# New instruction orders for PE, ACT, DVE and POOL in a fused gated-delta-attention and feed-forward kernel

## The chip, the cores and the metric

The kernel runs on one core of one Trainium2 chip. The time is that of the device from the first to the last instruction of one execution, in microseconds (us). PE is TensorE, ACT ScalarE, DVE VectorE, POOL GpSimd, SP SyncE. All engines run their own list of instructions in the order in which the kernel issues them, and meet through semaphores. Most matmuls are in float32.

## The reference

For x of shape (2, 4096, 512), with xn the layer norm of x over its last axis, the result is

`out = x + attention(xn) + ffn(xn)`

- **Attention** (4 heads of 128). q, k, v are projections of xn, each followed by a causal convolution of 4 taps and SiLU. beta is a sigmoid of a small projection. The delta rule works in chunks: with normalised k, the strictly lower triangle of k k^T scaled by beta is inverted, the state S is subtracted (y = v - k S), solved for u, and o = q S + (q k^T) u, S = S + k^T u.
- **Convolutions** of v over three lengths (3, 15 and 31 taps per channel), mixed by two matrices (ms_out).
- **Gates.** A two-layer network with GELU sees xn and the mean absolute values of ms_out, o and v, and gives a softmax over three parts. The weighted sum of ms_out, o and v is RMS-normalised and projected by Wo.
- **ffn.** sigmoid(xr Wr) * (relu(xk Wk)^2 Wv), where xr and xk mix xn with its predecessor in time.

## The kernel before, in words

**Tiles.** The sequence is cut into NS = 32 tiles of 128 time steps; a tile holds both batches (NB = 2, b = 0, 1), so most right-hand sides are 256 columns wide. All weights stay in SBUF.

**The loop.** `for i in range(NS + 2)` stands in each engine's program, with three flags: `f` (i < NS), `k` and `c` (i >= 2). In one turn, f works on tile i (layer norm, transposes `turn_x`, projections 0 to 3 of six pairs: v, v, k, k, q, q), k on tile i - 1 (projections 4 and 5, short convolutions, tap convolutions of heads 0 to 3, the inverse), c on tile i - 2 (the rest of the inverse, state, ffn, features, gates, output). A turn in the steady middle is called a stage here.

**The order.** No scheduler runs: each program ends in a list of calls of small helper functions, one list an engine, written out by hand or by a planner (PE from L681, ACT from L1170, DVE from L1550, POOL from L396). A helper waits for the semaphores that its operands and its destination need, issues a few instructions, and counts up its own semaphore. An engine that waits holds up all that stands behind it in its list.

**PE.** `inverse_W(l)` (L500, L504) and `inverse_Z(l)` (L521, L526, L528) build the inverse level by level: each has 64 matmuls of 32x32 by 16 columns, each of these with its own weight load. Between them DVE's `mask_W`, `step_Y` and `turn_Y` (L1426, L1434, L1438, L1415) must run. `inverse_W(0)` waits for `scale_B(1)` on ACT and for `make_aT(0)` on DVE, since it writes the bank `cell[0]` that `query_key(0)` (L483) has filled. `query_key(0)` waits for `scale_B(0)`. `kernel_mix(h)` (L614) multiplies the finished taps of head h; it waits for them and for `copy_mix(h - 1)`, which empties its bank. `key_state`, `solve`, `outputs`, `state` are L554, L561, L568 and L569, L575. `turn_features` (L631) turns the features for `hidden` (L645, L648) once `feature_low` (L1504, DVE) is done. `turn_x` is L426, `project` L439, `turn_o` L670, `attend` L678, `turn_tokens` L468.

**ACT.** `copy_beta` (L905), `tanh_beta` (copy L911, tanh L915), then DVE's `beta_half` and `gains` lead to `scale_B` (L931). `copy_logits` (L1123) empties the logits for `turn_logits` (L663); `exp_logits` (L1127) needs the Exp table. The features go `copy_ms(1)`, `feature_high` (L1093), DVE's `feature_rest` (L1498), `feature_mid` (L1099), `feature_low`. Silu (`short_silu`, L873), Gelu (`gelu_hidden`, L1116) and Exp each need a table; the compiler puts a load (ACT_TABLE_LOAD) where the table at hand does not hold the next function. `copy_raw` (L835) empties a projection's bank for the next but one.

**Taps.** Most taps are DVE instructions (`taps(s, h, lo, hi)`, L1488), some are products on ACT (`first_taps` L1054, `multiply_taps` L1065) that POOL adds by DMA (`add_taps`, L388). `first_taps(2)` waits for `kernel_mix(0)`. The first DVE tap of head 2 waits for `add_taps(2, 0)` to have landed, that of head 3 for `add_taps(3, 3)`.

**SP** loads the next x (L326, 512 KB) as soon as `turn_x(1)` of the tile before is done, and copies x to the output once the tile of two turns before has been stored.

Of the kernel before, what the change touches and what calls it, by code (L numbers as in the profile page):

```python
# [73 lines left out]
def build(nc, x, out, w):  # L74
    NS = x.shape[1] // P
    with ExitStack() as ctx:
# [271 lines left out]
        def pool_program(e):  # L348
# [47 lines left out]
            for i in range(NS + 2):  # L396
                f, k, c = i < NS, 1 <= i <= NS, i >= 2
                if f:
                    deviation(i)
                if k:  # L400
                    add_taps(i - 1, 2, 0)
                    add_taps(i - 1, 3, 0)
                    add_taps(i - 1, 3, 1)
                if c:
                    invert_o(i - 2, 0)
                    invert_o(i - 2, 1)
                if k:
                    add_taps(i - 1, 3, 2)
                    add_taps(i - 1, 3, 3)
                    norms_q(i - 1)  # L410
                    norms_k(i - 1)
                if c:
                    add_out(i - 2)

        def tensor_program(e):
# [265 lines left out]
            for i in range(NS + 2):  # L681
                f, k, c = i < NS, 1 <= i <= NS, i >= 2
                if c:
                    turn_tokens(i - 2, 3)
                    inverse_Z(i - 2, 5)
                    ffn_key(i - 2, 0)
                    half_W(i - 2)
                    ffn_key(i - 2, 1)
                    half_X(i - 2)
                    ffn_out(i - 2, 0)  # L690
                    solve(i - 2, 1)
                    key_state(i - 2, 0)
                    kernel_mix(i - 2, 2)
# [14 lines left out]
                if c:  # L708
                    turn_features(i - 2)
                    hidden(i - 2, 0)  # L710
                    hidden(i - 2, 1)
                if k:
                    turn_tokens(i - 1, 0)
                if c:
                    hidden(i - 2, 2)
# [9 lines left out]
                if k:  # L725
                    gram(i - 1, 0)
                if c:
                    turn_logits(i - 2)
                if k:
                    turn_beta(i - 1)  # L730
                    kernel_mix(i - 1, 0)
                    gram(i - 1, 1)
                    query_key(i - 1, 0)
                if f:
                    turn_x(i, 0)
                if k:
                    turn_tokens(i - 1, 2)
                    inverse_W(i - 1, 0)
                    query_key(i - 1, 1)
# [18 lines left out]
                if k:  # L758
                    inverse_Z(i - 1, 3)
                if f:  # L760
                    project(i, 3)
                if c:
                    turn_o(i - 2, 0)
                if k:
                    inverse_W(i - 1, 4)
                if c:
                    turn_o(i - 2, 1)
                    attend(i - 2, 0)
                if k:
                    inverse_Z(i - 1, 4)  # L770
                if c:
                    attend(i - 2, 1)
                if k:
                    inverse_W(i - 1, 5)

        def scalar_program(e):
# [393 lines left out]
            for i in range(NS + 2):  # L1170
                f, k, c = i < NS, 1 <= i <= NS, i >= 2
                if c:
                    relu_key(i - 2, 0)
                    copy_mix(i - 2, 1)
                    square_key(i - 2, 0)
                if k:
                    short_first(i - 1, 0)
                if c:
                    scale_v(i - 2, 1)
                if f:  # L1180
                    sum_x(i)
                if k:
                    copy_raw(i - 1, 2)
                if c:
                    relu_key(i - 2, 1)
                    square_key(i - 2, 1)
                    join_half_X(i - 2)
                    copy_u(i - 2, 1)
                if k:
                    short_first(i - 1, 1)  # L1190
                    take_raw_halo(i - 1, 3)
                    take_raw_halo(i - 1, 4)
                if c:
                    copy_u(i - 2, 0)
                    tanh_gate(i - 2, 0)
                if k:
                    odd_ones(i - 1)
                if c:
                    copy_o(i - 2, 0)
                    copy_o(i - 2, 1)  # L1200
                    copy_mix(i - 2, 2)
                    tanh_gate(i - 2, 1)
                if k:
                    copy_raw(i - 1, 3)
                if c:
                    copy_mix(i - 2, 3)
                if k:
                    short_first(i - 1, 2)
                    short_first(i - 1, 3)
                    take_raw_halo(i - 1, 5)  # L1210
                    short_silu(i - 1, 0)
                    copy_raw(i - 1, 4)
                    short_first(i - 1, 4)
                if f:
                    take_raw_halo(i, 0)
                if c:
                    copy_ms(i - 2, 0)
                    copy_ms(i - 2, 1)
                    feature_high(i - 2)
                    feature_mid(i - 2)  # L1220
                if k:
                    short_silu(i - 1, 1)
                    short_silu(i - 1, 2)
                    copy_raw(i - 1, 5)
# [11 lines left out]
                if k:  # L1236
                    shift(i - 1)
# [4 lines left out]
                if k:  # L1242
                    square_q(i - 1)
                if c:
                    gelu_hidden(i - 2, 2)
                if k:
                    multiply_taps(i - 1, 2, 0)
                    copy_tokens(i - 1, 1)
                if c:
                    gelu_hidden(i - 2, 3)  # L1250
                if f:
                    square_x(i)
                if c:
                    copy_logits(i - 2)
                if k:
                    copy_beta(i - 1)
                if c:
                    exp_logits(i - 2)
                if k:
                    tanh_beta(i - 1)  # L1260
                if f:
                    normalize(i, 0)
# [581 lines left out]
```

How the kernel before makes its waits and increments, by code:

```python
        def sync_program(e):  # L284
# [6 lines left out]
            def load_projections():  # L291
                load(v_in, wv[:, :, :], by_rows(w["wv"]))
                for j, n in enumerate(("cv", "ck", "cq")):
                    load(v_in, cw[:, j, :, :], w[n].rearrange("(c p) k -> p c k", p=P))
                load(k_in, wk[:, :, :], by_rows(w["wk"]))
                load(q_in, wq[:, :, :], by_rows(w["wq"]))
                e.wait_ge(zeroed, N_ZEROED)
                load(q_in, wb[:, :, 0:H], by_rows(w["wb"]))
# [24 lines left out]
            def load_x(s):  # L323
                if s:
                    e.wait_ge(*x_turned.upto(s - 1))
                e.dma_start(xa[:, :, :], x[:, s * P:(s + 1) * P, :].rearrange("b p d -> p b d")).then_inc(xa_in, 16)
# [1 line left out]
            def copy_x(s):  # L328
                if s >= 2:
                    e.wait_ge(stored[s % 2], s // 2 * 16)
                e.dma_start(out[:, s * P:(s + 1) * P, :], x[:, s * P:(s + 1) * P, :]).then_inc(x_copied[s % 2], 16)
# [3 lines left out]
            load_projections()  # L336
            load_convolutions()
            load_x(1)
            load_rest()
            for i in range(NS + 2):
                if 2 <= i < NS:
                    load_x(i)
                if 1 <= i <= NS:
                    copy_x(i - 1)
            for i in range(2):
                e.wait_ge(stored[i], NS // 2 * 16)
# [1 line left out]
        def pool_program(e):  # L348
# [2 lines left out]
                e.memset(t, 0.0).then_inc(zeroed, 1)  # L351
            e.wait_ge(zeroed, N_ZEROED)
            e.wait_ge(cst_in, 16)
```

## Time and profile before

| | us |
|---|---|
| median of 3 runs | 3585.44 |
| lowest, highest | 3582.49, 3594.63 |
| the profiled execution | 3585.26 |
| its span, first to last instruction | 3583.2 |
| PE busy in the span | 3454.6 (96%) |
| DVE busy | 3199.5 (89%) |
| ACT busy | 2765.0 (77%) |
| POOL busy | 423.0 (12%) |

How to read it: busy times are those of one execution. The time around the span is 2 us, so a change of the span is a change of the time. Matmuls overlap each other and their weight loads, so a row of n matmuls ends a little before start plus length, and the start of the next row is the better mark. "Idle before" is time in which the engine had nothing to run; "issue" means that no semaphore that the profile shows was behind it.

### The profile page before, as it was taken

The page shows a single profiled execution, that of the slowest core. Times are in us where ns is not written, and L with a number is a line of the kernel's source. Part 1 is how long each engine was busy: PE and PEld are TensorE (multiplying, and loading weights), DVE is VectorE, ACT ScalarE, POOL GpSimd, SP SyncE. Part 2 cuts the span into 40 slices and gives each one's busy share as a digit, 9 for nine tenths or more (in the row PEclk, how much of TensorE's full clock was granted, in tenths as well). Part 3 has the DMA queues.
Part 4 walks back from the last instruction along what each step waited for, and adds up shares of the span by engine and source line. Part 5 has one row for each costly group of instructions (what it writes and reads, how often), then busy time and mean ns, then how long its engine had stood idle before and what let it go on. Part 6 is the DMA issues. An engine that isn't in the chain of part 4 may idle for free. (4 is left out here: it accounts for less than half of the span.)

```text
span 3583.2 us, 97697 instructions
## 1 busy us (share of the span) xinstructions
PE 3454.6 (96%) x37184; PEld 2572.7 (72%) x37184; DVE 3199.5 (89%) x8208; ACT 2765.0 (77%) x9176; POOL 423.0 (12%) x497
## 2 busy tenths in 40 slices
PE   6999999999999999999999999999999999999986
PEld 5677777777777777777777777777777777777764
DVE  6998898998989999989999989989999998899983
ACT  5677887778887778887788877788877788777774
POOL 1011100111100111101111001111001110011110
PEclk9999999999999999999999999999999999999988
DMA  5022111122111122111221111221112221112110
GB/s 177 5 41 42 35 31 28 31 41 42 30 32 25 38 42 40 31 28 26 41 42 37 30 28 31 41 41 30 32 22 41 42 38 29 31 27 41 36 26 10
DMA packets 52204, 131.04 MB, mean 37 GB/s; under 512 B 9389, under 2 KB 9901, under 8 KB 51481
## 3 DMA queue, kind: packets, MB, share of 16 engines
q0 software_dynamic: 31744, 79.70, 12.9%
q1 hardware_dynamic: 19992, 45.10, 3.7%
q8 instruction: 294, 4.82, 0.6%
q14 instruction: 174, 1.42, 0.1%
HBM read 45.09 MB, written 33.55 MB: 22 GB/s over the span
## 5 line engine op out<-in xcount | busy, mean ns | idle before, releaser
L1488 DVE SCALAR_TENSOR_TENSOR my<-vT,mw,my 128x256 f32<-128x256 f32 x5408 | 2230.9, 480 | 105.6 <-ACT my L1054 69.9
L645 PE MATMUL dense<-xsh,w 128*128 128x256 f32 x2048 | 481.9, 381 | 1.3
L645 PEld LDWEIGHTS dense<-xsh,w 128*128 128x128 f32 x2048 | 368.3, 190 | 68.9 <-ACT xr L1116 8.3
L388 POOL DMA_DIRECT2D my<-prod x160 | 141.8, 886 | 964.6 <-ACT my L1054 498.4
L439 PE MATMUL front<-xsh,wk 128*128 128x256 f32 x1024 | 239.9, 387 | 3.4 <-ACT raw L835 3.4
L439 PE MATMUL front<-xsh,wv 128*128 128x256 f32 x1024 | 240.9, 388 | 0.8 <-ACT xsh L812 0.8
L586 PE MATMUL dense<-xk,wfk 128*128 128x256 f32 x1024 | 239.5, 387 | 0.0
L357 POOL TENSOR_SCALAR vare<-xsq 128x2 f32<-128x2 f32 x32 | 6.1, 192 | 1951.3 <-ACT xsh L797 1951.3
L678 PE MATMUL dense<-wo,ms 128*128 128x512 f32 x512 | 235.7, 604 | 0.0
L598 PE MATMUL dense<-wr,xr 128*128 128x512 f32 x512 | 233.7, 599 | 1.2 <-DVE xb L1471 1.2
L1065 ACT ACTIVATE prod<-vT,mw 128x256 f32<-128x256 f32 x480 | 210.3, 511 | 28.2 <-DMA my<-prod 27.9
L439 PE MATMUL front<-xsh,wq 128*128 128x256 f32 x1024 | 231.9, 379 | 0.0
L602 PE MATMUL dense<-wfv,ka 128*128 128x512 f32 x512 | 230.2, 592 | 0.0
L623 PE MATMUL dense<-cm,ym 128*128 128x512 f32 x512 | 225.0, 592 | 0.0
L439 PEld LDWEIGHTS front<-xsh,wq 128*128 128x128 f32 x1024 | 191.9, 190 | 38.8 <-issue 14.8
L990 ACT ACTIVATE Bm<-cell,g 128x128 f32<-128x128 f32 x256 | 73.0, 368 | 184.7 <-PE cell L561 184.7
L439 PEld LDWEIGHTS front<-xsh,wk 128*128 128x128 f32 x1024 | 190.1, 190 | 29.9 <-ACT raw L835 3.5
L439 PEld LDWEIGHTS front<-xsh,wv 128*128 128x128 f32 x1024 | 190.7, 191 | 27.9 <-issue 1.4
L586 PEld LDWEIGHTS dense<-xk,wfk 128*128 128x128 f32 x1024 | 190.3, 191 | 27.0
L614 PE MATMUL small<-my,km 128*128 128x256 f32 x768 | 201.8, 400 | 2.2 <-issue 2.2
L1054 ACT ACTIVATE my<-vT,mw 128x256 f32<-128x256 f32 x384 | 167.4, 507 | 36.2 <-PE small L614 35.9
L602 PEld LDWEIGHTS dense<-wfv,ka 128*128 128x128 f32 x512 | 97.2, 190 | 122.5 <-issue 108.6
(181 smaller groups left out, 6897.8 us busy)
## 6 DMA issues: line engine op xcount, KB each, us to landing
my<-prod POOLq DMA_DIRECT2D x160, 384.0 KB, 4.1
xa<-in_x SPq DMA_DIRECT2D x32, 512.0 KB, 4.2
out<-xb POOLq DMA_DIRECT2D x32, 512.0 KB, 5.9
w<-in_w SPq DMA_DIRECT2D x1, 2048.0 KB, 17.1
wv<-in_wv SPq DMA_DIRECT2D x1, 1024.0 KB, 6.6
wk<-in_wk SPq DMA_DIRECT2D x1, 1024.0 KB, 8.9
wq<-in_wq SPq DMA_DIRECT2D x1, 1024.0 KB, 8.4
wfk<-in_wfkT SPq DMA_DIRECT2D x1, 1024.0 KB, 7.1
```

The source lines that it names most:

```text
L388: e.dma_start(my[h % 2][:, :, :], prod[:, :, :], accum_op=ALU.add).then_inc(taps_added, 16)
L439: i = e.matmul(by_batch(front[pair % 2][:, c * W:(c + 1) * W]), wt[:, k, hs(c0 + c)], xsh[s % 2][:, k, :, 1:1 + P], start=(k == 0), stop=( ...
L586: i = e.matmul(dense[pair][:, c * W:(c + 1) * W], wfk[:, k, hs(2 * pair + c)], xk[:, k, :], start=(k == 0), stop=(k == CB - 1))
L598: i = e.matmul(dense[0][:, :], xr[:, k, hs(b)], wr[:, k, :], start=(k == 0), stop=(k == CB - 1))
L602: i = e.matmul(dense[1][:, :], ka[:, k, hs(b)], wfv[:, k, :], start=(k == 0), stop=(k == CB - 1))
L614: i = e.matmul(s_mix, km[:, p, :], my[h % 2][:, p, :], start=(p == 0), stop=(p == 2))
L623: i = e.matmul(dense[b][:, :], ym[:, k, hs(b)], cm[:, k, :], start=(k == 0), stop=(k == CB - 1))
L645: e.matmul(by_batch(o), w1[:, k, hs(2 * pair + c)], xsh[s % 2][:, k, :, 1:1 + P], start=(k == 0), stop=False)
L678: i = e.matmul(dense[b][:, :], ms[:, b, hs(h)], wo[:, h, :], start=(h == 0), stop=(h == H - 1))
L1054: i = e.activation(by_batch(my[h % 2][:, p, :]), vT[s % 2][:, c, :, VH - TAPS[j] + 1:VH - TAPS[j] + 1 + P], ACT.Copy, scale=mw[:, WOFF[j] ...
L1065: i = e.activation(by_batch(prod[:, p, :]), vT[s % 2][:, c, :, off:off + P], ACT.Copy, scale=mw[:, col:col + 1])
L1488: i = e.scalar_tensor_tensor(o, vT[s % 2][:, c, :, off:off + P], mw[:, col:col + 1], o, ALU.mult, ALU.add)
```

## The change

The same helpers are called in another order on PE, ACT, DVE and POOL; the helpers, their waits, the buffers and SP's list are the same. The part of the inverse from `inverse_Z(5)` to `half_X`, `ffn_key` and `ffn_out(0)` are called at the end of a turn for tile i - 1, no more at the start of the next one for tile i - 2. `norms_q` is called for tile i - 2 at the start of POOL's turn. Some runs of `taps` are cut or joined in other places; each tap is still called once a tile. Below are POOL and PE whole, ACT from `short_first(2)` to the end of the turn, and three places of DVE, with 12 columns of indentation taken off.

```diff
@@ -395,19 +395,22 @@
 
 for i in range(NS + 2):
     f, k, c = i < NS, 1 <= i <= NS, i >= 2
+    if c:
+        norms_q(i - 2)
     if f:
         deviation(i)
     if k:
         add_taps(i - 1, 2, 0)
         add_taps(i - 1, 3, 0)
+    if c:
+        invert_o(i - 2, 0)
+    if k:
         add_taps(i - 1, 3, 1)
-    if c:
-        invert_o(i - 2, 0)
+        add_taps(i - 1, 3, 2)
+    if c:
         invert_o(i - 2, 1)
     if k:
-        add_taps(i - 1, 3, 2)
         add_taps(i - 1, 3, 3)
-        norms_q(i - 1)
         norms_k(i - 1)
     if c:
         add_out(i - 2)
@@ -681,16 +684,9 @@
 for i in range(NS + 2):
     f, k, c = i < NS, 1 <= i <= NS, i >= 2
     if c:
-        turn_tokens(i - 2, 3)
-        inverse_Z(i - 2, 5)
-        ffn_key(i - 2, 0)
-        half_W(i - 2)
-        ffn_key(i - 2, 1)
-        half_X(i - 2)
-        ffn_out(i - 2, 0)
+        kernel_mix(i - 2, 2)
+        key_state(i - 2, 0)
         solve(i - 2, 1)
-        key_state(i - 2, 0)
-        kernel_mix(i - 2, 2)
         solve(i - 2, 0)
     if k:
         project(i - 1, 4)
@@ -708,10 +704,10 @@
     if c:
         turn_features(i - 2)
         hidden(i - 2, 0)
+    if k:
+        turn_tokens(i - 1, 0)
+    if c:
         hidden(i - 2, 1)
-    if k:
-        turn_tokens(i - 1, 0)
-    if c:
         hidden(i - 2, 2)
     if k:
         turn_tokens(i - 1, 1)
@@ -723,25 +719,22 @@
         logits(i - 2, 0)
         logits(i - 2, 1)
     if k:
+        turn_beta(i - 1)
         gram(i - 1, 0)
+        turn_tokens(i - 1, 2)
     if c:
         turn_logits(i - 2)
     if k:
-        turn_beta(i - 1)
-        kernel_mix(i - 1, 0)
         gram(i - 1, 1)
         query_key(i - 1, 0)
+        kernel_mix(i - 1, 0)
+        inverse_W(i - 1, 0)
     if f:
         turn_x(i, 0)
-    if k:
-        turn_tokens(i - 1, 2)
-        inverse_W(i - 1, 0)
+        turn_x(i, 1)
+    if k:
+        inverse_W(i - 1, 1)
         query_key(i - 1, 1)
-    if f:
-        turn_x(i, 1)
-    if k:
-        inverse_W(i - 1, 1)
-        key_state(i - 1, 1)
         inverse_Z(i - 1, 1)
         kernel_mix(i - 1, 1)
         inverse_W(i - 1, 2)
@@ -757,21 +750,31 @@
         project(i, 2)
     if k:
         inverse_Z(i - 1, 3)
+    if c:
+        turn_o(i - 2, 0)
+    if k:
+        key_state(i - 1, 1)
+    if c:
+        attend(i - 2, 0)
+    if k:
+        inverse_W(i - 1, 4)
     if f:
         project(i, 3)
     if c:
-        turn_o(i - 2, 0)
-    if k:
-        inverse_W(i - 1, 4)
-    if c:
         turn_o(i - 2, 1)
-        attend(i - 2, 0)
     if k:
         inverse_Z(i - 1, 4)
+        turn_tokens(i - 1, 3)
     if c:
         attend(i - 2, 1)
     if k:
         inverse_W(i - 1, 5)
+        ffn_key(i - 1, 0)
+        inverse_Z(i - 1, 5)
+        ffn_key(i - 1, 1)
+        half_W(i - 1)
+        ffn_out(i - 1, 0)
+        half_X(i - 1)
 
         def scalar_program(e):
 e.wait_ge(zeroed, N_ZEROED)
@@ -1169,151 +1172,160 @@
...
         short_first(i - 1, 2)
+        take_raw_halo(i - 1, 5)
         short_first(i - 1, 3)
-        take_raw_halo(i - 1, 5)
         short_silu(i - 1, 0)
+    if c:
+        copy_ms(i - 2, 0)
+    if k:
         copy_raw(i - 1, 4)
+        short_silu(i - 1, 1)
         short_first(i - 1, 4)
-    if f:
-        take_raw_halo(i, 0)
-    if c:
-        copy_ms(i - 2, 0)
+    if c:
         copy_ms(i - 2, 1)
         feature_high(i - 2)
         feature_mid(i - 2)
-    if k:
-        short_silu(i - 1, 1)
+    if f:
+        take_raw_halo(i, 0)
+    if k:
+        take_v_halo(i - 1)
         short_silu(i - 1, 2)
+    if c:
+        copy_features(i - 2)
+    if k:
         copy_raw(i - 1, 5)
-    if c:
-        copy_features(i - 2)
-    if k:
-        take_v_halo(i - 1)
         short_first(i - 1, 5)
+        short_silu(i - 1, 3)
         first_taps(i - 1, 0)
-        short_silu(i - 1, 3)
         short_silu(i - 1, 4)
         short_silu(i - 1, 5)
     if c:
         gelu_hidden(i - 2, 0)
     if k:
-        shift(i - 1)
         first_taps(i - 1, 1)
         copy_tokens(i - 1, 0)
     if c:
         gelu_hidden(i - 2, 1)
     if k:
         square_q(i - 1)
+        copy_tokens(i - 1, 1)
+        multiply_taps(i - 1, 2, 0)
     if c:
         gelu_hidden(i - 2, 2)
-    if k:
-        multiply_taps(i - 1, 2, 0)
-        copy_tokens(i - 1, 1)
-    if c:
         gelu_hidden(i - 2, 3)
+    if k:
+        copy_beta(i - 1)
     if f:
         square_x(i)
+    if k:
+        tanh_beta(i - 1)
     if c:
         copy_logits(i - 2)
     if k:
-        copy_beta(i - 1)
-    if c:
-        exp_logits(i - 2)
-    if k:
-        tanh_beta(i - 1)
+        scale_B(i - 1, 0)
+        scale_B(i - 1, 1)
     if f:
         normalize(i, 0)
-    if k:
-        scale_B(i - 1, 0)
+        normalize(i, 1)
+    if k:
         first_taps(i - 1, 2)
-        scale_B(i - 1, 1)
+    if c:
+        exp_logits(i - 2)
     if f:
-        normalize(i, 1)
         copy_xnT(i, 0)
-    if c:
-        weigh_delta(i - 2, 0)
+        copy_xnT(i, 1)
     if k:
         copy_mix(i - 1, 0)
     if c:
         weigh_ms(i - 2, 0)
-    if f:
-        copy_xnT(i, 1)
-    if c:
-        weigh_delta(i - 2, 1)
     if k:
         multiply_taps(i - 1, 3, 0)
         first_taps(i - 1, 3)
     if c:
-        weigh_v(i - 2, 0)
-        weigh_ms(i - 2, 1)
-        weigh_v(i - 2, 1)
-        square_o(i - 2, 0)
+        weigh_delta(i - 2, 0)
     if f:
         take_raw_halo(i, 1)
-    if k:
-        multiply_taps(i - 1, 3, 1)
+    if c:
+        weigh_v(i - 2, 0)
+        weigh_delta(i - 2, 1)
     if f:
         copy_raw(i, 0)
     if c:
-        square_o(i - 2, 1)
+        square_o(i - 2, 0)
+    if k:
+        multiply_taps(i - 1, 3, 1)
+    if c:
+        weigh_ms(i - 2, 1)
+        normalize_o(i - 2, 0)
+    if k:
+        copy_tokens(i - 1, 2)
+    if c:
+        weigh_v(i - 2, 1)
+        copy_oT(i - 2, 0)
     if f:
         copy_raw(i, 1)
     if k:
+        multiply_taps(i - 1, 3, 2)
+    if c:
+        square_o(i - 2, 1)
+    if k:
         mix_half(i - 1)
-        multiply_taps(i - 1, 3, 2)
-    if f:
-        take_raw_halo(i, 2)
-    if c:
-        normalize_o(i - 2, 0)
+    if c:
         normalize_o(i - 2, 1)
-        copy_oT(i - 2, 0)
+    if k:
+        multiply_taps(i - 1, 3, 3)
+    if c:
         copy_oT(i - 2, 1)
     if k:
-        multiply_taps(i - 1, 3, 3)
-        copy_tokens(i - 1, 2)
-        copy_W(i - 1)
         spread_X(i - 1)
-        join_X(i - 1)
-        copy_tokens(i - 1, 3)
-        scale_v(i - 1, 0)
-        copy_half_W(i - 1)
@@ -1554,76 +1566,87 @@
     if i == 2:
         prepare_weights()
     if c:
+        taps(i - 2, 3, 0, 2)
+        taps(i - 2, 3, 3, 4)
+        taps(i - 2, 3, 2, 3)
+        taps(i - 2, 2, 48, 49)
+        taps(i - 2, 3, 5, 6)
+        taps(i - 2, 3, 4, 5)
...
-        taps(i - 2, 3, 30, 31)
+        taps(i - 2, 3, 32, 34)
+        taps(i - 2, 3, 35, 37)
+        gate_value(i - 2, 0)
+        subtract_state(i - 2, 0)
+        taps(i - 2, 3, 39, 40)
         taps(i - 2, 3, 38, 39)
-        taps(i - 2, 3, 40, 41)
-        taps(i - 2, 3, 33, 34)
-        taps(i - 2, 3, 41, 42)
-        subtract_state(i - 2, 0)
-        taps(i - 2, 3, 36, 37)
...
+        taps(i - 2, 3, 72, 78)
+    if k:
+        short_conv(i - 1, 0)
+    if c:
+        gate_value(i - 2, 1)
+    if k:
+        short_conv(i - 1, 1)
+        short_conv(i - 1, 2)
     if f:
         negate_mean(i)
-    if c:
-        taps(i - 2, 3, 47, 48)
-        taps(i - 2, 3, 43, 44)
-        taps(i - 2, 3, 42, 43)
-        taps(i - 2, 3, 50, 51)
-        taps(i - 2, 3, 45, 47)
-        taps(i - 2, 3, 48, 50)
-        taps(i - 2, 3, 51, 52)
-        taps(i - 2, 3, 53, 55)
-        taps(i - 2, 3, 52, 53)
-        taps(i - 2, 3, 56, 57)
...
```

## Rows read from the trace of the kernel before

**Rows 1.** The page: busy time of each engine, and the queue of instructions.
```profile
PE 3454.6 (96%) x37184; PEld 2572.7 (72%) x37184; DVE 3199.5 (89%) x8208; ACT 2765.0 (77%) x9176; POOL 423.0 (12%) x497
...
q8 instruction: 294, 4.82, 0.6%
```

**Rows 2.** Windows: length, busy us of each engine (count), granted clock, DMA share, GB/s.
```profile
177.26:3447.56 3270.30, 3218.25 (x34861) 2398.82 (x34861) 2986.78 (x7679) 2586.70 (x8601) 392.60 (x448) 1.00 0.17 34
944.28:1051.58 107.30, 106.68 (x1162) 79.63 (x1163) 99.44 (x257) 86.18 (x288) 13.22 (x15) 1.00 0.17 35
286.13:398.18 112.05, 109.76 (x1162) 81.83 (x1162) 99.92 (x257) 86.31 (x288) 13.18 (x15) 0.97 0.17 33
292.94:299.76 6.82, 6.52 (x141) 5.25 (x141) 4.88 (x13) 2.75 (x8) 0.00 (x0) 0.50 0.13 49
```

**Rows 3.** Waits of PE: for whom, us in total, times, longest us.
```profile
PE cell L521 <- issue: 15.6, 14, 1.4
...
PE cell L500 <- issue: 12.1, 16, 1.5
PE cell L483 <- ACT Bm L931: 11.8, 32, 0.6
```

**Rows 4.** Timeline of PE in one steady stage: start, us, instruction, [idle before].
```profile
2030.89 1.16 PE L483 MATMUL cell<-qT,kT 128*128 128x128 f32 x8 [0.36 <-ACT Bm L931]
...
2033.11 0.73 PE L500 MATMUL cell<-cst,Bm 32*32 32x16 f32 x64 [0.19 <-ACT Bm L931]
...
2035.95 1.16 PE L554 MATMUL cell<-S,kT 128*128 128x128 f32 x8
...
2047.81 0.73 PE L500 MATMUL cell<-Yq,Bm 32*32 32x16 f32 x64
```

**Rows 5.** Timeline of PE: gaps inside groups of matmuls, in two stages.
```profile
293.24 1.86 PE L554 MATMUL cell<-S,kT 128*128 128x128 f32 x7 [1.68 <-issue]
...
1927.86 0.36 PE L500 MATMUL cell<-Yq,Bm 32*32 32x16 f32 x20 [0.95 <-issue]
...
1932.14 0.49 PE L500 MATMUL cell<-Yq,Bm 32*32 32x16 f32 x35 [0.33 <-issue]
```

**Rows 6.** Timeline of ACT: table loads and beta's tanh, first and steady stage.
```profile
33.70 1.28 ACT L873 ACT_TABLE_LOAD   x1
...
52.76 0.21 ACT L915 ACTIVATE bt<-bq 128x8 f32<-128x8 f32 x1
...
2027.29 1.28 ACT L1127 ACT_TABLE_LOAD   x1
...
2028.90 0.21 ACT L915 ACTIVATE bt<-bq 128x8 f32<-128x8 f32 x1
```

**Rows 7.** Timelines of ACT, DVE and PE around the features.
```profile
2007.61 0.72 ACT L873 ACTIVATE vT<-vT 128x256 f32<-128x256 f32 x2
...
2007.73 0.23 DVE L1504 TENSOR_TENSOR fparts<-frest,fparts 128x72 bf16<-128x72 f32 x1 [0.32 <-ACT fparts L1099]
...
2008.16 0.27 PE L631 MATMUL small<-ident,fparts 128*108 128x128 bf16 x2
```

**Rows 8.** Timelines of POOL and DVE: issue of add_taps(2,0), first tap that needs it.
```profile
2032.33 0.94 POOL L388 DMA_DIRECT2D my<-prod  x1 [4.49 <-ACT my L1054]
...
2036.59 1.27 DVE L1488 SCALAR_TENSOR_TENSOR my<-vT,mw,my 128x256 f32<-128x256 f32 x3
...
399.61 0.94 POOL L388 DMA_DIRECT2D my<-prod  x1 [4.49 <-ACT my L1054]
...
405.59 1.28 DVE L1488 SCALAR_TENSOR_TENSOR my<-vT,mw,my 128x256 f32<-128x256 f32 x3 [0.24 <-DMA my<-prod]
```

**Rows 9.** Timelines of ACT, PE and DVE in the first turn with k.
```profile
75.52 1.31 ACT L1065 ACTIVATE prod<-vT,mw 128x256 f32<-128x256 f32 x3 [9.30 <-DMA my<-prod]
...
77.41 5.41 PE L439 MATMUL front<-xsh,wk 128*128 128x256 f32 x16 [3.40 <-ACT raw L835]
...
83.53 0.29 DVE L1438 TENSOR_TENSOR Yq<-Yq,cell 128x128 f32<-128x128 f32 x1 [4.98 <-PE cell L521]
```

More of the change, by code:

```diff
@@ L714, in tensor_program @@
                 if c:
+                    hidden(i - 2, 1)
                     hidden(i - 2, 2)
@@ L743, in tensor_program @@
                     inverse_W(i - 1, 1)
-                    key_state(i - 1, 1)
+                    query_key(i - 1, 1)
                     inverse_Z(i - 1, 1)
@@ L1198, in scalar_program @@
                 if c:
+                    scale_v(i - 2, 1)
+                if k:
+                    copy_raw(i - 1, 2)
+                    short_first(i - 1, 1)
+                if c:
+                    copy_half_W(i - 2)
+                if k:
+                    take_raw_halo(i - 1, 3)
+                if c:
+                    relu_key(i - 2, 1)
+                    copy_mix(i - 2, 1)
+                if k:
+                    shift(i - 1)
+                    take_raw_halo(i - 1, 4)
+                if c:
+                    square_key(i - 2, 1)
+                    tanh_gate(i - 2, 0)
+                    scale_v(i - 2, 0)
+                    join_half_X(i - 2)
+                    copy_u(i - 2, 1)
+                    copy_mix(i - 2, 2)
+                    copy_u(i - 2, 0)
                     copy_o(i - 2, 0)
                     copy_o(i - 2, 1)
-                    copy_mix(i - 2, 2)
-                    tanh_gate(i - 2, 1)
                 if k:
@@ L1205, in scalar_program @@
                 if c:
+                    tanh_gate(i - 2, 1)
                     copy_mix(i - 2, 3)
@@ L1702, in vector_program @@
                 if k:
+                    taps(i - 1, 2, 10, 11)
+                    taps(i - 1, 2, 17, 18)
+                    taps(i - 1, 2, 15, 16)
+                    taps(i - 1, 2, 13, 14)
+                    step_Y(i - 1, 2)
+                    taps(i - 1, 2, 20, 21)
+                    turn_Y(i - 1, 3)
+                    taps(i - 1, 2, 18, 19)
+                    taps(i - 1, 2, 23, 24)
+                    taps(i - 1, 2, 21, 22)
+                    taps(i - 1, 2, 24, 25)
                     taps(i - 1, 2, 16, 17)
+                    taps(i - 1, 2, 26, 27)
+                    mask_W(i - 1, 3)
                 if c:
@@ L1734, in vector_program @@
                     taps(i - 1, 2, 33, 34)
+                    step_Y(i - 1, 3)
+                    taps(i - 1, 2, 36, 37)
                     taps(i - 1, 2, 40, 41)
+                    turn_Y(i - 1, 4)
+                    taps(i - 1, 2, 41, 42)
+                    taps(i - 1, 2, 31, 32)
+                    taps(i - 1, 2, 42, 43)
+                    mask_W(i - 1, 4)
+                    taps(i - 1, 2, 43, 44)
                     mix_in(i - 1)
-                    taps(i - 1, 2, 41, 42)
+                    step_Y(i - 1, 4)
+                    taps(i - 1, 2, 44, 45)
                     taps(i - 1, 2, 34, 35)
-                    turn_Y(i - 1, 4)
-                    mask_W(i - 1, 4)
-                    taps(i - 1, 2, 42, 43)
-                    taps(i - 1, 2, 36, 37)
-                    taps(i - 1, 2, 43, 45)
+                    taps(i - 1, 2, 45, 46)
+                    taps(i - 1, 2, 37, 38)
+                    taps(i - 1, 2, 46, 47)
+                    turn_Y(i - 1, 5)
                 if c:
```

253 lines of the change are left out of this document (112 added, 141 removed).

## The prediction, made before the changed kernel ran

> **What bounds the kernel now.** The page's first part says TensorE: PE is busy 96% of the span, DVE 89%, ACT 77% [rows 1]. The windows then say how full PE is where it matters. A stage is one turn of the loop over i; the 30 from 177.26 to 3447.56 take 3270.30 us with 3218.25 of PE work [rows 2]: 109.0 us a stage. The undisturbed stage from 944.28 takes 107.30 with 106.68 of PE work, the one from 286.13 takes 112.05 for the same 1162 matmuls. So a new order can win at most what stands between PE's work and the stage, not the matmuls' own time; and DVE and ACT, with 99.4 and 86.2 us of work a stage, are not the bound unless PE has to wait for one of them.
>
> PE's list of waits says what stands there [rows 3]. Two waits come in each stage: query_key(0) for scale_B(0), 11.8 us in 32 [rows 3], and inverse_W(0) for scale_B(1); read in a stage they are 0.36 and 0.19 [rows 4], 0.55 us together. The others are "issue": 15.6 us in 14 and 12.1 us in 16 on the 32x16 matmuls, with two smaller groups some 35 us, or 1.1 a stage. These stop in the middle of a group that no semaphore guards. The queue of kind "instruction" moved 4.82 MB in 294 packets [rows 1], so one packet is 16.4 KB, and PE's 74,368 instructions over 294 are 253: a packet is some 256 of them. Between the two gaps of one stage, at 1927.86 and 1932.14, lie 127 matmuls, each with its weight load, and a few waits: 256 again [rows 5]. So I read the gaps as PE running out of instructions. There it used up 256 in 4.0 us and then waited 0.33: a packet takes about 4.3 us to come, and only where inverse_W and inverse_Z put 128 instructions into 0.7 us [rows 4] is PE faster than that. Behind the gap of 1.68 us at 293.24 the granted clock is 0.50 (1.2 of 2.4 GHz) from 292.94 to 299.76 [rows 2, 5].
>
> The Trainium skill ("Runtime: NRT & Kernel Launch", Instruction fetch mechanics) has the fetch of the next 256 instructions mostly hidden, with PE's buffer at 2048; by that a denser order costs nothing and (f) below would be 0; the gaps of this trace speak against it.
>
> **The change, part by part.** No instruction, wait or buffer is added. Much of the diff is where the loop's body is cut: ffn_key, half_W, ffn_out(0), half_X move from the top of one turn to the bottom of the one before, which is the same place. I compare the order as a cycle. Costs are per steady stage, times 30.
>
> (a) *The beta chain.* copy_beta and tanh_beta now stand ahead of copy_logits and exp_logits, turn_beta ahead of gram(0), scale_B(1) ahead of first_taps(2). Before, the table load at 2027.29 (1.28 us) stood in front of tanh_beta at 2028.90, because exp_logits did [rows 6]. Without it, with square_x (1.4) in its place, beta's tanh comes at about 2027.4, scale_B(0) ends at 2029.05 and scale_B(1), no more behind 1.2 us of first_taps, at 2030.1. query_key(0) is ready for them at 2029.6, inverse_W(0) after kernel_mix(0) at 2032.0. Both waits go: -0.55 x 30 = -16.5 us. This rests on tanh needing no table load behind Gelu. No row shows tanh there; rows show it without a load behind Exp (2028.90) and behind Silu (52.76, the last load at 33.70) [rows 6], so I take none. Bounds: none, or 0.9 us of wait per stage (rival 3).
>
> (b) *short_silu(1) moves ahead of copy_ms(1)*, so ahead of the features; take_raw_halo(0) (0.1) goes behind. Features run on ACT without a gap and are 0.62 - 0.1 = 0.52 later, as silu(1) begins now after them at 2007.61 and takes 0.62. feature_low ended at 2007.96 and turn_features began on PE at 2008.16 [rows 7]: 0.20 of slack, less 0.06 for the semaphore. PE then waits 0.38 us in each stage; nothing else is ready, since project(5) is used up. +11.4. Bounds 0 to 0.5.
>
> (c) *kernel_mix(1) behind copy_mix(0).* kernel_mix(0) went from before gram(1) to after query_key(0) and ends at 2032.0; first_taps(2) waits for it (1.3), then the exp table load (1.28), two copy_xnT (1.0) and copy_mix(0): done at 2036.05. PE comes to kernel_mix(1) at 2035.9, having lost key_state(1) (1.1 [rows 4]) from the stretch. +0.2: +6. Bounds 0 to 0.5.
>
> (d) *Near ties.* solve(0) has only solve(1) (0.89) to cover subtract_state(0) (0.69 plus 0.25 of semaphores), kernel_mix(3) has one more tap ahead of it, attend(0) comes 0.1 before copy_oT(0). 0.25 together: +7.5. Bounds 0 to 0.5.
>
> (e) *The tap additions.* DVE's first tap of head 2 needs add_taps(2,0) landed. Before, POOL issued it at 2032.33 and DVE used it without a wait at 2036.59 (4.26 or less); in another stage issue to tap was 5.98 with DVE waiting (399.61 to 405.59) [rows 8]. Now first_taps(2) ends 1.4 later, so the issue is at 2033.7, and turn_x(1) starts x's 512 KB load at the same time, not 3 us later: both on the same engines. From the landing to inverse_W(3), DVE has 17 taps at 0.4 (three in 1.28 [rows 8]), mask_W(2), add_two, add_three and step_Y(2): 8.4 us. inverse_W(3) stood at 2047.81 [rows 4] and is due at 2046.2 now, 12.5 after the issue, so the landing may take 4.1. Between 4.2 and 6.0 the wait is 0.1 to 1.9, less the 1.1 us that PE loses to instructions in the same stretch anyway. I take 0.5: +15. Bounds 0 and 1.9 x 30.
>
> (f) *Instruction supply.* The dense stretch loses key_state(1) and the two waits, but kernel_mix(0) stands close ahead and turn_x(0) and (1) are inside it. I laid 256-instruction windows over both orders with the durations above: the shortest holds 2.2 us of work in both. +0.1: +3. Bounds -0.3 to +0.5 a stage, the falls of the clock with it: the stage with the gap of 1.68 is 4.75 longer than the undisturbed one [rows 2], so 3 us of it are the clock's.
>
> (g) *Both ends.* In the first stage with k, multiply_taps(3,1) waits 9.30 us for a DMA, copy_raw(0) stands behind it, so PE waits 3.40 and DVE 4.98 [rows 9]. copy_raw(0) is ahead now, and DVE, which bounds this stage up to solve(0), gains 4. In the last two turns weigh, square and normalize of batch 0 go ahead of batch 1: 1 us off the end, and 1 in the stage without f, which DVE's length sets. -6. Bounds -10 to 0. POOL's norms_q goes behind add_out and is due only at copy_o of the next turn; SP issues the same transfers in the same order.
>
> Sum: -16.5 + 11.4 + 6 + 7.5 + 15 + 3 - 6 = +20.4. The profiled execution took 3585.26 us (span 3583.2), the median of the runs 3585.44, so both bases agree: about **3605 us**.
>
> **The rivals.**
> 1. *Faster.* If (b) to (e) are covered, as (e) is where the add lands in 4.1 us and (b) where ACT is half a microsecond ahead, only (a) and (g) stay: 3585.3 - 22.5 = 3563. For it: four of my terms are differences of two long sums that come out within 0.5 us. Against: (b) is a plain shift against a slack that is read directly. It decides at 0.2 us of delay of the features. Chance 0.25.
> 2. *No change.* PE's supply of instructions sets the stretch: what the two waits no longer take, the next packet takes, and the tap additions hide in the same gap. Then (a) and (e) are 0, (b) and (g) stay with half of (c) and (d): about +10, or 3590 with its neighbours 3577 to 3595. That from project(4) to hidden(0) PE's order as a cycle is the old one, so that the change does less than the diff's length says, speaks for it too; against it, (b) lies outside the dense stretch. Chance 0.32.
> 3. *A table load in front of tanh_beta.* Then copy_logits comes at 2029.05, turn_logits, now ahead of gram(1), waits 0.9 us: +27 on the sum, 3632. Against it are the rows of (a). Chance 0.08, inside slower. 
>
> **How the numbers follow.** The forecast (slower by over 0.3%, 10.8 us, about what a measurement can tell) has 0.43 with rival 3, no change 0.32, faster 0.25. The low end is rival 1's 3563, with 0.1 us a stage of (b) to (e) left: 3566. The high end is the sum with (e) at 1.2 and (c), (d) at 0.4: 3605 + 21 + 6 + 5 = 3637, rounded to 3640.
>
> **What would show it.** (a): no wait of query_key(0) or inverse_W(0) for ACT's scale_B, 96 table loads as before with the Exp one at exp_logits. (b): turn_features waits for DVE's feature_low in each stage, 0.3 to 0.5. (c): kernel_mix(1) waits for copy_mix. (e): DVE's waits for the tap DMA grow from 28.8 us to over 40, and inverse_Z(2) or inverse_W(3) waits for DVE. (f): issue gaps stay near 35 us. (g): no wait of 3.4 us for copy_raw in the first stage. The prediction is wrong if PE's waits in a steady stage sum to under 0.55 us, or if issue gaps leave the range of 25 to 50.

## The result and the profile after

The changed kernel takes **3628.44 us** (median of 6 runs, 3622.01 to 3633.99) against 3585.06 (6 runs) for the kernel before: ratio **1.0119**, 95% interval 1.0103 to 1.0134, so 43 us slower. Forecast were 3605, with 3566 to 3640 as range. The profiled execution took 3630.37 us, its span is 3628.6.

Page of the changed kernel, busy time of each engine [rows 1] (lines of the kernel's file are some 3 to 12 higher than before):

```profile
PE 3466.4 (96%) x37184; PEld 2569.2 (71%) x37184; DVE 3205.2 (88%) x8208; ACT 2787.0 (77%) x9176; POOL 468.6 (13%) x497
```

The work is the same; PE's 12 us more go with a lower mean granted clock, 0.983 against 0.987. Waits of PE [rows 3]: for whom, us in total, times, longest:

```profile
PE cell L524 <- DVE Wq L1438: 39.9, 20, 11.5
PE cell L503 <- issue: 30.5, 19, 2.9
...
PE cell L503 <- DVE Yq L1450: 10.6, 16, 3.8
PE small L617 <- issue: 8.6, 1, 8.6
...
PE small L617 <- ACT ym L1075: 4.3, 13, 0.4
...
PE small L634 <- DVE fparts L1516: 3.3, 2, 3.0
```

The 8.6 us at L617 are one wait of kernel_mix before the first outputs, from 121.26 to 129.82 us. No packet of q8, the queue of instructions, starts in it. DVE is in its taps all that time and ends one at 129.72. So it is most likely a wait for taps that the profile gives no semaphore for:

```profile
117.76 12.36 DVE L1500 SCALAR_TENSOR_TENSOR my<-vT,mw,my 128x256 f32<-128x256 f32 x31
```

The two waits for scale_B are gone. In their place inverse_Z waits for mask_W (L1438), inverse_W for step_Y (L1450). DVE's own waits name what stands behind both (28.8 us in 37 before, 2.3 the longest):

```profile
DVE my L1500 <- DMA my<-prod: 80.7, 37, 12.6
```

Where the time went, from the first matmul of outputs(0) in each turn: the first comes at 139.22 us (130.69 before), the last at 3552.47 (3508.38), the end at 3628.57 (3583.18). So the head costs 8.5 us more, the 31 turns between 35.6 (1.15 each), the tail 1.3.

Within a stage I took each of PE's calls from its first matmul to that of the next call, averaged over 27 stages. This step also holds waits that the idle column shows only in part, as matmuls in flight cover them. Worked out from PE's rows, in us:

| step of PE | before | after | first run below | what follows it |
|---|---|---|---|---|
| project(0) | 3.66 | 4.96 | 3.82 | inverse_Z(2), waits for mask_W(2) |
| inverse_W(2) | 0.93 | 1.67 | 1.14 | "issue" inside it |
| project(1) | 3.66 | 4.10 | 3.76 | inverse_W(3), waits for step_Y(2) |
| project(5) | 3.46 | 3.72 | 3.72 | turn_features |
| gram(1) | 1.42 | 0.97 | 0.97 | query_key(0), waited for scale_B(0) |
| turn_tokens(2) | 0.79 | 0.44 | 0.44 | before: inverse_W(0), waited for scale_B(1) |
| whole stage | 109.02 | 110.36 | 108.47 | |

One stage shows the mechanism. Timelines of SP, POOL, DVE and PE of the changed kernel, then its DMA view for the same two issues (last column: median us from issue to landing):

```profile
2395.32 0.38 SPq L326 DMA_DIRECT2D xa<-in_x  x1
...
2395.49 0.93 POOL L388 DMA_DIRECT2D my<-prod  x1 [5.33 <-ACT my L1057]
...
2398.90 0.45 DVE L1427 STREAM_TRANSPOSE Xq<-Yq 128x256 f32<-128x256 f32 x1
2401.31 3.25 DVE L1500 SCALAR_TENSOR_TENSOR my<-vT,mw,my 128x256 f32<-128x256 f32 x8 [1.97 <-DMA my<-prod]
2404.49 0.28 DVE L1438 TENSOR_TENSOR Wq<-cell,cst 128x128 f32<-128x128 f32 x1
...
2403.00 0.25 PE L503 MATMUL cell<-Yq,Bm 32*32 32x16 f32 x7 [2.78 <-issue]
```

```profile
xa<-in_x SPq DMA_DIRECT2D x1, 512.0 KB, 4.1
my<-prod POOLq DMA_DIRECT2D x1, 384.0 KB, 5.7
```

SP and POOL issue within 0.2 us of each other, but SP's packets go first. In the kernel before, the addition issued at 2032.33 [rows 8] landed after 4.0 us by the same view, as the x load came 4.1 us behind it. The records of the packets say how: the x load runs from 2396.35 to 2399.05, the addition from 2398.39 to 2400.93, and while both run the addition's packets in progress rise from 1 to 17 as the load's fall from 15 to none. Over 27 stages the addition's first packet starts 2.96 us after the issue, never under 2.49; without a load in front it is 1.51. Its last packet ends 5.81 us after the issue instead of 4.39, and the semaphore that DVE waits for tells of the landing at 6.18 instead of 4.77 (means). DVE waits 2.2 us a stage for it instead of 0.4. (The expectations below go by 5.8 against 4.2, and by waits of 2.17 against 0.32.)

The Trainium skill ("DMA: Bandwidth & Descriptors", Queues, rings and completion order) has each DMA engine take turns between queues, but drain a whole packet of some 9 to 17 descriptors first. The trace fits this: the load is 272 records, which is 17 for each of 16 engines, and the addition's begin only as the load's run out. The records do not name their engine, so that each engine finishes its 17 first is not shown.

### The profile page after: what moved, and what is told of

Read it like the earlier page. It is cut to its first block, busy times and chain, and to the rows that moved or that the text cites. A ratio compares the mean times of both kernels' runs of the same rounds, so it can differ in the third digit from the quotient of the medians.

```text
span 3628.6 us, 97702 instructions
## 1 busy us (share of the span) xinstructions
PE 3466.4 (96%) x37184; PEld 2569.2 (71%) x37184; DVE 3205.2 (88%) x8208; ACT 2787.0 (77%) x9176; POOL 468.6 (13%) x497
## 3 DMA queue, kind: packets, MB, share of 16 engines
q14 instruction: 173, 1.42, 0.1%
## 4 chain that ended last, share of the span: by engine, by line
PE 71%; ACT 13%; DMA 6%; issue 5%; DVE 4%; ACTq 0%; POOL 0%; POOLq 0%; DVEq 0%; SPq 0%
PE dense L648 12%; PE front L442 11%; PE dense L681 6%; PE dense L601 6%; PE dense L589 6%; PE dense L605 6%; DMA my<-prod 6%; DVE my L1500 3%; PE small L617 3%; PE cell L479 2%; ACT dense L1087 2%; PE turn L471 2%; PE cell L564 2%; PE cell L578 2%; PE cell L572 2%
## 5 line engine op out<-in xcount | busy, mean ns | idle before, releaser
L442 PE MATMUL front<-xsh,wv 128*128 128x256 f32 x1024 | 258.8, 409 | 4.0 <-issue 3.2
L442 PEld LDWEIGHTS front<-xsh,wv 128*128 128x128 f32 x1024 | 203.5, 204 | 36.2 <-issue 4.4
L617 PE MATMUL small<-my,km 128*128 128x256 f32 x768 | 198.9, 395 | 14.7 <-issue 8.6
L626 PEld LDWEIGHTS dense<-cm,ym 128*128 128x128 f32 x512 | 94.8, 190 | 107.1 <-issue 107.1
```

The costliest lines, as they stand in the source:

```text
L442: i = e.matmul(by_batch(front[pair % 2][:, c * W:(c + 1) * W]), wt[:, k, hs(c0 + c)], xsh[s % 2][:, k, :, 1:1 + P], start=(k == 0), stop=( ...
L617: i = e.matmul(s_mix, km[:, p, :], my[h % 2][:, p, :], start=(p == 0), stop=(p == 2))
L626: i = e.matmul(dense[b][:, :], ym[:, k, hs(b)], cm[:, k, :], start=(k == 0), stop=(k == CB - 1))
```

## The experiments

All are timed against the kernel before; the ratio is given with its 95% interval.

### The x load behind the addition

The changed kernel with one wait more, on SP:

```diff
 def load_x(s):
     if s:
         e.wait_ge(*x_turned.upto(s - 1))
+    if s >= 2:
+        e.wait_ge(*adds_before(s - 2, 2, 1))
     e.dma_start(xa[:, :, :], ...)
```

> The new orders, with one wait more on SP: the load of tile s's x also waits until add_taps(2,0) of tile s-2 has landed. Theory T (collision): in the new orders the x load is issued 0.9 us after the issue of add_taps(2,0), so its packets go first, the add lands 5.8 us after its issue and not 4.2, DVE's first tap of head 2 waits 2.17 us a stage and not 0.32, and the head loses 8.5 us in the same way. By T the add lands within 3.9 us again, DVE's waits for the tap DMA fall from 80.7 to under 35 us, PE's waits for DVE's mask_W from 39.9 to under 12, and the time from 3628 to 3570-3585. Rival 1 (features, near ties and the denser instruction stream carry the loss): 3615-3630, whatever DVE waits. Rival 2 (only the head is the collision's): 3618-3622.

Measured: **3561.72 us**, ratio 0.994 (0.9928 to 0.9952), 67 us faster than the changed kernel (64 by the two ratios) and 22 faster than the one before. Waits of PE and DVE, and the DMA view of one addition:

```profile
PE cell L505 <- issue: 16.4, 16, 1.5
...
PE cell L505 <- DVE Yq L1452: 7.0, 6, 4.2
...
PE cell L526 <- DVE Wq L1440: 4.5, 4, 2.5
...
DVE my L1502 <- DMA my<-prod: 15.3, 30, 1.4
```

```profile
my<-prod POOLq DMA_DIRECT2D x1, 384.0 KB, 4.1
```

The addition begins 1.51 us after its issue, its last packet ends after 3.89 and it lands after 4.27 (means). The 31 turns lose 56.4 us of length and the head 7.3 (first outputs at 131.88), so it is the same cause at both places. The time is below the range that I gave: the collision costs 1.8 us a turn, where the difference to the kernel before was 1.15, as it had also eaten a gain of the new orders.

### The x load two additions later

The same wait with `adds_before(s - 2, 3, 2)`.

> As the run before, but the x load waits for the landing of add_taps(3,1), two additions later, so that it falls between two additions and behind the dense stretch of the inverse. If only add_taps(2,0) matters (T): the same as the run before within 5 us. If the x load slowed PE's instruction packets or add_taps(3,0) as well, another 5-15 us faster. If ACT's sum_x of the next turn comes to wait for x (it is due 38 us after the turn's first addition, the load would land some 25 us after it), slower than the run before.

Measured: **3552.60 us**, ratio 0.9914 (0.99 to 0.9928). Another 9 us by the medians, in the bounds given, but the two intervals touch. The profiles show only part of it, and not the part that was put: the head is 3.6 us shorter (first outputs at 128.29), while the 31 turns take as long as in the run before it (3357.4 against 3356.9). PE's "issue" waits sum to 25 us against 32, but that is one wait of kernel_mix in the head (2.6 us, not 8.5); after the first outputs they are 22.1 against 23.2. So the turns show no gain from fewer waits for instructions.

### The same wait on the old orders

> Control: the kernel before, its orders untouched, with the wait of the second run alone (the x load waits for the landing of add_taps(3,1)). Theory T: in the kernel before the x load's packets came 4.1 us after the issue of add_taps(2,0), in the shadow of the addition, and DVE waited only 0.32 us a stage; so this gains 0 to 8 us, 3576-3584, and what the second run won over the kernel before is the new orders' own. Rival: the x load disturbs additions and instruction packets in both kernels, and the second run's gain is the later load's alone: 3550-3562.

Measured: 3584.16 us, ratio 1.0003 (0.9993 to 1.0014). That is the upper edge of what was put. DVE's wait for the additions stays at 32.3 us (28.8 before). The later load by itself is worth nothing; what the two runs above won is the new orders' own.

### The collision on the old orders

The kernel before, its addition held back until the event that releases the x load; and the same with the x load behind the addition.

```diff
 def add_taps(s, h, r):
+    if (h, r) == (2, 0) and s + 1 < NS:
+        e.wait_ge(*x_turned.upto(s + 1))
     e.wait_ge(*tap_zero.upto(s, h))
```

> The converse, on the kernel before: POOL's add_taps(2,0) also waits until turn_x(1) of the same turn is done, the event that releases SP's x load. Nothing else changes. The addition is then issued some 2 us later than before and 0.9 us ahead of the x load's packets, as in the new orders. Theory T (position): it begins 2.7-3.1 us after its issue and lands 5.5-6.0 after it, so 7.5-8 after the old issue instead of 4.2; DVE's wait grows from 0.32 to over 3 us a stage, and the time by 1.5 to 3 us a stage, 3630-3680. Rival (in the old orders the landing has slack enough, so the collision alone costs little): below 3610.

> The run before it with the x load waiting for that addition's landing: the same delay of the issue, without the collision. Theory T: it lands 3.7-3.9 us after its issue, 2 us less than in the run before, and 1 to 2 us a stage come back: 30-60 us faster than that run. Rival (the delay of the issue is all that counts): within 10 us of that run.

Measured: **3720.90** us (1.0392, 1.0374 to 1.041) and **3644.15** (1.0176, 1.0158 to 1.0194); the first and the difference of both are larger than put, though the addition starts 2.52 us after its issue, a little sooner than put. DVE waits 4.9 us a stage for it in the first and 3.5 in the second. Both additions are issued at the same late event, so the 77 us between them are the collision's. The first is 141 us slower than the kernel before, so the delay of the issue costs the other 65. DVE's and PE's waits of the first, then of the second:

```profile
PE cell L502 <- DVE Yq L1440: 125.4, 32, 13.4
...
DVE my L1490 <- DMA my<-prod: 168.6, 48, 14.5
```

```profile
PE cell L504 <- DVE Yq L1442: 72.4, 32, 3.3
...
DVE my L1492 <- DMA my<-prod: 113.7, 42, 4.3
```

Here PE waits for step_Y on DVE (L1440, L1442), which stands behind the tap that needs the addition. An addition that ends 1.5 us later (its last packet 5.53 against 4.05 us after the issue) makes PE's wait for step_Y 53 us longer in 32 turns, and the mean granted clock falls from 0.984 to 0.973 with it.

### The addition made small

The changed kernel; add_taps(2,0) moves `[:, 0:1, 0:16]` of the tile, so most of one product of head 2 is left out.

> The new orders with the early x load as they are, but add_taps(2,0) moves 64 bytes a partition instead of 3072 (it leaves out most of that one addition of products, so the sums of head 2 are incomplete). It tells position from bandwidth. If the addition is late because its packets stand behind those of the x load (position): it still begins 2.5 to 3.1 us after its issue instead of 1.5, lands at 3.2-3.7, DVE's wait shrinks from 2.17 to 0.1-0.3, and the time is 3555-3570. If the addition is late because two transfers share the engines (bandwidth): it begins 1.5 us after its issue. If the landing is not what costs, 3615-3630. Issue gaps of 2.2 to 2.9 us in inverse_W(2) should go in any case if a PE packet stood behind the addition's bytes.

Measured: 3551.72 us, ratio 0.9913 (0.9893 to 0.9934), 3 us below the range put; DVE waits 0.4 us a stage. Waits of PE, and the DMA view of the 32 small additions:

```profile
PE cell L504 <- issue: 11.3, 14, 1.3
...
PE small L618 <- issue: 8.5, 1, 8.5
...
PE cell L525 <- DVE Wq L1439: 3.5, 3, 2.5
```

```profile
my<-prod POOLq DMA_DIRECT2D x32, 8.0 KB, 3.9
```

Even with 64 bytes a partition the first packet starts 2.63 us after the issue (mean of 27; 1.51 in the last two turns, where no x is loaded). So it stands behind the load; its last packet ends after 3.60 us. And the gaps of over 2 us in inverse_W are gone, 1.3 at most: in the changed kernel PE's 16 KB packet of instructions ran from 2400.78 to 2401.76, from the time that the addition's last packets ended (2400.93), and PE went on at 2403.00, 1.24 us after it had come. In this kernel nothing long stands in front of it.

### DVE's inverse steps ahead of the taps

The changed kernel; on DVE mask_W(2) moves up 5 taps and step_Y(2) 4, both still behind the tap that waits.

> The new orders with the early x load and its late addition as they are; on DVE alone mask_W(2) goes 5 taps up and step_Y(2) 4 taps up, both still behind the tap that waits for the addition. If the late landing costs because mask_W(2) and step_Y(2) stand 8 and more taps behind it on DVE: DVE's wait for the addition stays at 2 us a stage, but PE's waits for mask_W fall from 39.9 to under 12 us, and the time to 3575-3600. If PE loses time to the collision in another way (packets of instructions behind the addition, the clock): over 3605, and issue gaps as in the new orders, 45 us.

Measured: 3617.46 us, ratio 1.0102 (1.0083 to 1.0121). That is 11 us under the changed kernel's median, but its interval overlaps that one's (1.0103 to 1.0134), so a gain is not clear of the noise. The time is in the second expectation (over 3605); the waits for mask_W fall, but not to under 12. PE's waits:

```profile
PE cell L503 <- issue: 29.1, 19, 2.7
PE cell L524 <- DVE Wq L1438: 24.5, 18, 9.3
```

The step of project(0) falls from 4.96 to 4.10, but inverse_W(2) stays at 1.71 and project(2) grows by 0.37. So this order on DVE shortens one wait and gives a part of it back at another, and the waits for instructions in inverse_W stay (29.1 against 30.5 us).

### The same, with the late x load

mask_W(2) 2 taps up, on the second run.

> The second run (late x load) with mask_W(2) 2 taps up on DVE. PE waited there 5.4 us in all for mask_W and 16 for instructions in inverse_W. If these are what is left to order: 3-5 us faster than the second run's 3552.6. If DVE then waits for inverse_W(2) instead: the same within 4 us, or slower.

Measured: 3552.18 us, ratio 0.9923 (0.9906 to 0.994): the same as without it.

### The short silu

The changed kernel, and the second run, with one call moved on ACT:

```diff
     copy_raw(i - 1, 4)
-    short_silu(i - 1, 1)
...
+    short_silu(i - 1, 1)
     take_v_halo(i - 1)
     short_silu(i - 1, 2)
```

> The new orders with one call moved on ACT: short_silu(1) goes back behind feature_mid, in front of take_v_halo. Prediction's term (b): 0.25 to 0.38 us a stage, so 7.5 to 11.4 us faster than the new orders, 3617-3621; the step from project(5) to turn_features falls back from 3.72 to 3.46 us. Rival: the DVE wait for the tap addition later in the stage takes it back (the additions hang on ACT too, which would be as late as now): 3625-3630.

> The second run with short_silu(1) back behind feature_mid, so term (b) alone without the collision. In the third run PE's step at project(5) fell by 0.26 us but the one at hidden(1) grew by 0.38, as hidden(2) then waits for gelu_hidden(0). If ACT's work from copy_ms to gelu_hidden(0) is the bound of that stretch whatever its order: the same as the second run within 5 us (3548-3558). Prediction's term (b) as it was put: 8 to 11 us faster, 3542-3545.

Measured: 3628.08 us (1.0125, 1.0112 to 1.0138) and 3559.79 (0.9936, 0.9921 to 0.9952): no gain in either; beside the second run the second one is 7 us slower, and their intervals just overlap. A new line stands among PE's waits of the first:

```profile
PE dense L648 <- ACT xr L1119: 6.4, 30, 0.4
```

The step of project(5) falls from 3.72 to 3.46 as put, but hidden(1)'s grows from 3.69 to 4.06: hidden(2) now waits for gelu_hidden(0) (L1119). All of it, the silu and the features, stands in front of that gelu on ACT.

### The beta chain alone, on the old orders

> The kernel before with the beta chain alone in the new order: copy_beta and tanh_beta ahead of copy_logits and exp_logits, scale_B(1) ahead of first_taps(2), turn_beta ahead of gram(0), turn_tokens(2) in front of turn_logits, exp_logits behind normalize(1), softmax_top and softmax_rest later on DVE. kernel_mix(0), the features and the short silu stay. Prediction's term (a): the waits of query_key(0) and inverse_W(0) for scale_B go, 0.55 us x 30 = 16.5 us, 3565-3572. Rival (supply of instructions): PE runs into the next packet earlier by what it gained, 3580-3588 with issue gaps grown by 10 us or more. Second rival: first_taps(2) comes later (0.9 us) behind scale_B(1), the addition with it, and DVE's waits for the tap DMA grow by over 10 us: 3580-3595.

> The beta chain alone on the kernel before, mended: copy_logits stays ahead of copy_beta and softmax_top ahead of beta_half, so that the bank of the logits is empty for kernel_mix(0) as before. Only exp_logits goes behind normalize(1), scale_B(1) goes ahead of first_taps(2), turn_beta ahead of gram(0), softmax_rest behind mask_W(1), and the two copy_xnT ahead of weigh_delta. Term (a): the 0.55 us a stage of waits for scale_B go, 3565-3573. Rival (instruction supply takes it back): 3580-3586 with the issue gaps grown by some 10 us. Rival (first_taps(2) is 0.9 us later and with it the addition): up to 3590, DVE's waits for the tap DMA over 45 us.

Measured: **3747.82** us (1.0455, 1.044 to 1.0471) and **3660.01** (1.0219, 1.0203 to 1.0235). None of the expectations came, in either run. PE's waits of the first, then of the second:

```profile
PE small L614 <- DVE lg L1514: 88.3, 31, 2.9
PE front L439 <- ACT raw L835: 31.6, 23, 2.2
```

```profile
PE front L456 <- ACT bqT L905: 34.7, 32, 2.5
PE front L439 <- ACT raw L835: 24.3, 18, 4.2
```

In the first, kernel_mix(0) waits for the bank that turn_logits has filled and softmax_top has not yet emptied. In the second, turn_beta (L456) waits for copy_beta, behind square_x and copy_logits on ACT. So neither way of moving the chain alone gives its gain. My reading, which no run took apart: copy_beta first makes the logits late, these need turn_tokens(2) as cover, and kernel_mix(0) must go behind them. That kernel_mix(0) in turn makes first_taps(2) and the addition late.

### The beta chain undone, on the new orders

The second run; on ACT copy_logits and exp_logits in front of tanh_beta, on DVE softmax_top in front of beta_half.

> Term (a) undone on the second run (new orders, late x load): on ACT copy_logits and exp_logits, with its table load, go back in front of tanh_beta, and softmax_top back in front of beta_half on DVE; PE's order stays the new one. If the beta chain is what makes the new orders faster than the old without the collision (31 us in the second run, where the prediction gave (a) 16.5): scale_B(0) ends some 1.3 to 2 us later in each stage, and all or more of the gain goes, 3575-3620, with PE waiting for scale_B in each stage. If the gain lies elsewhere (neighbours of small groups on PE, the ends): 3550-3560.

Measured: 3638.01 us, ratio 1.0158 (1.0137 to 1.0178), 85 us slower than the second run and past the range.

```profile
PE cell L488 <- ACT Bm L936: 61.5, 32, 2.2
```

The step of gram(1) is 3.10 us, not 0.97: query_key(0) waits for a scale_B(0) that has exp_logits in front, with its table load (1.28 us) and its wait for softmax_top. The gain of the new orders hangs on this chain.

## Why the prediction went wrong in size

**Right:** slower, inside the range; and the collision in (e) was named with its cause, x's load at the same time as the addition. That the time is inside the range is in part luck: two errors of opposite sign stand in the sum. The collision was put at 15 us and cost 67 (the first run gives them back), and all the rest was put at +5.4 and is -22, the first run against the kernel before.

- **(e), the term that failed.** The prediction took 0.5 us a stage between bounds of 0 and 1.9. The landing was foreseen between 4.2 and 6.0 us after the issue and came after 6.2 in the mean of 27 stages, 5.7 at the least: the load is always first, and the addition starts as it runs out. By the prediction's own line (the landing may take 4.1) that is a wait of 2.1, "less the 1.1 us that PE loses to instructions in the same stretch anyway". This subtraction is the step that failed. The 1.1 are no cover: PE's packet comes behind the same addition and is later with it; the "issue" waits after the first outputs are 37.5 us with the collision and 23.2 without. The steps of project(0), project(1) and inverse_W(2) cost 1.30 + 0.44 + 0.74 = 2.5 us a stage. Taking the cause away gives back 67 us, 1.8 a turn and 7.3 in the head: close to the upper bound.
- **(a)** was right, and larger: the steps of gram(1) and turn_tokens(2) shrink by 0.45 + 0.35 = 0.80 us where the idle rows showed 0.55; undoing the chain costs 85 us. Tanh behind Gelu needs no load, so rival 3 did not come.
```profile
L1119 ACT ACT_TABLE_LOAD x32 | 41.1, 1283 | 0.6
L1130 ACT ACT_TABLE_LOAD x32 | 41.1, 1283 | 0.6
L876 ACT ACT_TABLE_LOAD x31 | 39.8, 1283 | 0.6
```

- **(b)** has its price, 0.25 us at project(5) instead of 0.38, but it is no loss against another place of the silu, as the two runs show.
- **(c)** did not come: kernel_mix(1)'s step fell from 1.86 to 1.53 us, its waits for copy_mix are 4.3 us in all. **(d)** about as put: solve, kernel_mix(3) and attend(0) are 0.34 longer together, against 0.25.
- **(f)** "Issue" waits are 46 us, not near 35, inside the range of 25 to 50; 8.6 of them are kernel_mix's in the head. After the first outputs they are 37.5 us against 34.2 before, with nine gaps of over 2 us against one. Without the collision they are 23.2, so the new orders alone lose less to them than the old. The length of instruction windows did not foresee either; what grew is the time that a packet takes behind an addition.
- **(g)** Wrong in sign: for the head -4 foreseen and +8.5 measured, for the end -2 foreseen and +1.3 measured behind the last outputs. The timelines of SP, POOL and DVE show why:

```profile
61.69 0.42 SPq L326 DMA_DIRECT2D xa<-in_x  x1
62.16 0.65 SPq L332 DMA_DIRECT2D out<-in_x  x1
...
61.66 1.09 POOL L388 DMA_DIRECT2D my<-prod  x1 [7.51 <-ACT my L1057]
...
77.77 3.26 DVE L1500 SCALAR_TENSOR_TENSOR my<-vT,mw,my 128x256 f32<-128x256 f32 x8 [12.58 <-DMA my<-prod]
```

  SP's copy of x to the output (L332) follows the load at once. By the packet records it runs until 77.18, and the addition's last packets end with it, single ones 2.7 us apart. The wait of 3.4 for copy_raw is gone as put, and with the collision away the first outputs come at 128.29 in the second run, 2.4 earlier than before.

The 3563 of rival 1 is near what the new orders take without the collision, 3561.72, but not for its reasons: (b) and (d) are there, (a) is larger, and (g) gives nothing (head 1.2 us and tail 1.8 us longer than before in the first run). And rival 2's own parts, (b), (g) and half of (c) and (d), sum to +12 or 3597, not to the 3590 that it gives. Of the further 0.6 us a stage that the new orders win (turn_tokens(0) and (3), key_state(1), each 0.15 to 0.33 less), the cause was not tried.

## What to carry to other kernels

Where two queues' transfers come due together, don't price the overlap as shared bandwidth: look which is issued first, and let the one behind start only when the other's packets run out (1.1 to 1.5 us later here). Move the one that nobody waits for: the x load is first read 36 to 39 us after its issue, and one wait on the idle SP was worth 67 us. And a wait measured on an engine is no cover for a second one that hangs on the same queue. The best orders here are the new ones with the load behind add_taps(3,1), 0.9914 of the kernel before.

## What the hardware showed that I had not expected

- An engine's packets of instructions can come late behind data. In all eight gaps of 2.2 us and more in the changed kernel's steady stages, the packet started in the last microsecond of an addition, and PE went on 1.2 to 1.5 us after it had landed. With the addition made small the "issue" waits after the first outputs fall from 37.5 to 15.8 us. Which DMA engine carried a packet is not in the records. The Trainium skill ("Runtime: NRT & Kernel Launch", Instruction fetch mechanics) has this fetch mostly hidden. In this trace 32 "issue" waits after the first outputs, 37.5 us in all, are not, beside some 290 packets.
- A transfer of 8 KB behind one of 512 KB starts 1.1 us later than alone (2.63 against 1.51 after the issue).
- In or just behind six of these eight gaps the granted clock goes to the lower level (1.2 of 2.4 GHz), as in the kernel before [rows 2, 5]; here for 3.4 us (window of the changed kernel: length, busy us of PE, PEld, DVE, ACT, POOL, clock, DMA share, GB/s):

```profile
2403.20:2406.60 3.40, 3.40 (x13) 2.77 (x9) 3.40 (x10) 3.40 (x13) 0.85 (x1) 0.50 0.38 70
```
